# Staging rows of a decayed-attention layer: interleaved rows with flat stores, maxima in two transfers, and a layer norm one step earlier

## Reference

```
x = x + 0.5 * moe(layernorm(x))      # 8 experts, the best 2
x = x + attention(layernorm(x))      # 16 heads of 8 features
x = x + 0.5 * moe(layernorm(x))

# attention, per head: q, k, v = x@Wq, x@Wk, x@Wv
c      = cumsum(log_sigmoid(x @ Wf))          # one number per head and token
scores = q k^T * 8**-0.5 + c[i] - c[j], causal
out    = softmax(scores) @ v, heads joined, @ Wo
```

## Time and profile before

| | us |
|---|---|
| median of 3 runs | 488.97 |
| lowest, highest | 486.0, 489.73 |
| the profiled execution, its own time | 487.24 |
| its span, first to last instruction | 485.5 |
| PE busy in the span | 416.7 |
| DVE busy | 372.5 |
| ACT busy | 278.3 |
| POOL busy | 239.7 |

### The profile page before, as it was taken

The page is one execution under the profiler, slowest core; times in us unless marked ns, Lnnn a source line. Parts: engine busy times, 40 slices in busy tenths (PEclk is TensorE's granted clock), DMA queues, the critical chain, the costliest instruction groups (busy, mean ns, idle before and its releaser), DMA issues.

```text
span 485.5 us, 12085 instructions
## 1 busy us (share of the span) xinstructions
PE 416.7 (86%) x3472; PEld 303.6 (63%) x3488; DVE 372.5 (77%) x1316; ACT 278.3 (57%) x758; POOL 239.7 (49%) x397
## 2 busy tenths in 40 slices
PE   1888887847799999999999999999989999888884
PEld 0656566526556766676676676676667666566662
DVE  4999999874856865876785686676576658999995
ACT  5676766440354555565556466455555685666753
POOL 8955566351425534533543543553442543566554
PEclk9999999895989999999999999999999999999999
DMA  3311000033333333234233233323322000001101
GB/s 108 92 52 20 1 0 1 8 99 109 101 98 101 94 100 115 73 96 114 69 104 102 85 96 100 100 84 98 111 77 80 4 3 0 24 24 32 33 22 43
DMA packets 29402, 32.47 MB, mean 67 GB/s; under 512 B 2312, under 2 KB 26140, under 8 KB 29370
## 3 DMA queue, kind: packets, MB, share of 16 engines
q1 hardware_dynamic: 28282, 31.57, 22.1%
q10 hardware_dynamic: 1088, 0.52, 0.4%
HBM read 16.05 MB, written 15.20 MB: 64 GB/s over the span
## 4 chain that ended last, share of the span: by engine, by line
PE 40%; DVE 22%; DMA 19%; issue 10%; ACT 3%; POOL 3%; DVEq 1%; SPq 1%; ACTq 0%; POOLq 0%; another core or an unknown queue 0%
DMA a_q_rows<-a_max_t 16%; PE bank L847 10%; PE bank L862 7%; DVE m_lower L288 7%; PE bank L877 6%; PE bank L850 3%; PE bank L968 2%; PE bank L960 2%; PE bank L963 2%; DVE m_stats L335 2%; DMA q_stage<-a_q_parts 2%; POOL m_pair L216 2%; DVE x_all L297 2%; DVE m_best_no L376 2%; PE bank L886 1%
## 5 line engine op out<-in xcount | busy, mean ns | idle before, releaser
L773 DVE TENSOR_REDUCE a_neg_max<-bank 128x2 f32<-128x512 f32 (+1 forms) x192 | 124.3, 687 | 76.2 <-PE bank L850 70.2
L712 ACT ACTIVATE a_weights<-bank 128x512 f32<-128x512 f32 x192 | 108.4, 592 | 60.5 <-PE bank L862 55.6
L658 POOL TENSOR_SCALAR_AFFINE_SELECT a_weights<-a_weights 128x512 f32<-128x512 f32 (+1 forms) x96 | 75.7, 790 | 127.9 <-ACT a_weights L712 127.7
L847 PE MATMUL bank<-a_k_rows,a_q_rows 104*128 104x256 f32 (+1 forms) x512 | 100.9, 321 | 7.7 <-DMA a_k_rows<-k_stage 6.5
L847 PEld LDWEIGHTS bank<-a_k_rows,a_q_rows 104*128 104x128 f32 x512 | 78.9, 199 | 26.9 <-issue 18.5
L246 ACT ACTIVATE m_scaled<-bank,m_gates 128x128 f32<-128x128 f32 x256 | 72.6, 367 | 25.0 <-PE bank L417 25.0
L862 PE MATMUL bank<-a_q_rows,a_k_rows 106*128 106x512 f32 (+1 forms) x192 | 69.8, 442 | 11.1 <-DMA a_q_rows<-a_max_t 10.5
L216 POOL TENSOR_TENSOR m_pair<-m_scaled 128x256 f32<-128x256 f32 x64 | 48.3, 755 | 60.4 <-ACT m_scaled L246 60.1
L288 DVE SCALAR_TENSOR_TENSOR m_lower<-bank,m_gates,m_lower 128x128 f32<-128x128 f32 x192 | 66.1, 344 | 1.2
L877 PE MATMUL bank<-a_weights,a_v 128*32 128x128 f32 x1536 | 61.6, 279 | 0.0
L850 PE MATMUL bank<-a_mask,a_ident 128*128 128x256 bf16 (+1 forms) x176 | 56.4, 321 | 0.0
(11 more groups left out here) (126 smaller groups left out, 784.0 us busy)
## 6 DMA issues: line engine op xcount, KB each, us to landing
a_k_rows<-k_stage SPq DMA_DIRECT2D x16, 416.0 KB
k_stage<-a_k_parts SPq DMA_DIRECT2D x48, 128.0 KB
q_stage<-a_q_parts SPq DMA_DIRECT2D x48, 128.0 KB
a_q_rows<-q_stage SPq DMA_DIRECT2D x64, 96.0 KB
x_all<-in_L_attn_x SPq DMA_DIRECT2D x8, 256.0 KB, 2.8
out_x<-x_all SPq DMA_DIRECT2D x8, 256.0 KB, 2.3
we<-in_L_ffn_We SPq DMA_DIRECT2D x1, 512.0 KB, 4.0
k_stage<-a_c_parts SPq DMA_DIRECT2D x32, 16.0 KB
```

What stands on the lines that cost most here:

```text
L658: nc.gpsimd.affine_select(out=diagonal, in_=diagonal, compare_op=ALU.is_ge, fill=0.0, base=0, pattern=[[0, heads.stop - heads.start], [1, P]],
L712: nc.scalar.activation(weights[n // 2 % 3][:, half:half + 4, :].rearrange("p h n -> p (h n)"), wt_bank[n % 2][:, :], ACT.Exp).then_inc(wt_ ...
L773: nc.vector.tensor_reduce(neg_max[:, t, first:first + heads], score_bank[p % 2][:, :].rearrange("p (h n) -> p h n", h=heads), AX.X, ALU.ma ...
L847: nc.tensor.matmul(bank[:, n * keys:(n + 1) * keys], q_rows[b][0:KR, h, t * P:(t + 1) * P], k_rows[b][0:KR, h % NU, 0:keys], start=n == 0, ...
```

## The change

1. **Layout.** The staging tensors have the row outermost and the group second, and rows of the groups are interleaved in `q_rows` and `k_rows` (row r of group g is partition 4r + g). The weights Wq and Wk are reordered to match (d, g, u instead of g, d, u). A store is then 128 partitions to one flat piece of DRAM, a c store 16 partitions to one flat piece. The loads of `q_rows` write every fourth partition. Sizes and numbers of stores and loads stay.
2. **Maxima.** `send_max` issues two DMAs, one for each of the two rows, each from 16 partitions (16 heads). The waits count 32 in place of 16.
3. **Layer norm.** Statistics and power of a sequence move from part 0 of step s to part 3 of step s-1, `xn` from part 1 to part 4 of step s-1. Sequence 0 stays where it was. In part 3 of DVE's list the statistics stand behind the two row maxima and ahead of L813 and `normalise`; in part 4 `xn` stands behind the two row maxima, ahead of L819 and L821. POOL's power stands behind `causal` of part 3.
4. **xT.** In part 2 ACT's copy to `xt` stands ahead of exp number 4.
5. **Loop.** For all engines but SP the loop is three rounds (steps 2 to 10); steps 11 to 13 are written out.

```diff
-    run_steps(..., 0, seqs - 1, (2, 2 + (seqs - 4) // 3 * 3), 3)
+    run_steps(..., 0, seqs - 1, (2, 2 + (seqs - 5) // 3 * 3), 3)
...
-    q_dram = nc.dram_tensor("q_stage", (3, NG, 3 * HD, NU, N), FP32, kind="Internal").ap()
-    k_dram = nc.dram_tensor("k_stage", (3, NG, ROWS, NU, N), FP32, kind="Internal").ap()
+    q_dram = nc.dram_tensor("q_stage", (3, 3 * HD, NG, NU, N), FP32, kind="Internal").ap()
+    k_dram = nc.dram_tensor("k_stage", (3, ROWS, NG, NU, N), FP32, kind="Internal").ap()
...
-                    sp.dma_start(raw(q_rows[b])[ROWS * g:ROWS * g + 3 * HD, NU * g:NU * (g + 1), :],
-                                 q_dram[b, g]).then_inc(rows_in, 16)
+                    sp.dma_start(raw(q_rows[b])[g:NG * 3 * HD:NG, NU * g:NU * (g + 1), :],
+                                 q_dram[b, :, g]).then_inc(rows_in, 16)
...
-                    sp.dma_start(k_dram[b, :, r * HD:(r + 1) * HD].rearrange("g d u n -> g (d u) n"),
+                    sp.dma_start(k_dram[b, r * HD:(r + 1) * HD].rearrange("d g u n -> (d g u) n"),
                                  raw(k_parts)[:, part, :]).then_inc(k_stored, 16)
...
-                    sp.dma_start(k_dram[b, :, 3 * HD + part], raw(c_parts)[:, part, :]).then_inc(c_stored, 16)
+                    sp.dma_start(k_dram[b, 3 * HD + part].rearrange("g u n -> (g u) n"), raw(c_parts)[:, part, :]).then_inc(c_stored, 16)
...
-            if j == 0 and 0 <= s + 2 < NSEQ:
-                n = i + 3
-                pool.wait_ge(eps_done, n)
-                nc.gpsimd.tensor_tensor(rstd[:, :], var_eps[:, :], c["minus_half"][:, 0:2], ALU.pow).then_inc(rstd_done, 1)
+            if s == -2 and j == 0:
+                rstd_of(i + 3)
+            if j == 3 and 0 <= s + 3 < NSEQ:
+                rstd_of(i + 4)
...
-            act.dma_start(raw(q_rows[s % 3])[KR:KM, :, t * P:(t + 1) * P], raw(max_t[t])).then_inc(max_in[t], 16)
+            for k in range(2):
+                act.dma_start(raw(q_rows[s % 3])[KR + k:KR + k + 1, :, t * P:(t + 1) * P],
+                              raw(max_t[t])[k * H:(k + 1) * H, :]).then_inc(max_in[t], 16)
...
-            if X:
-                exp(i - 1, s - 1, 2 * j)
             if j == 2 and F:
                 act.wait_ge(xt_ready, n)
                 nc.scalar.activation(xt[:, :], proj_bank[:, 0:N], ACT.Copy).then_inc(xt_copied, 1)
+            if X:
+                exp(i - 1, s - 1, 2 * j)
...
+            if s == -2 and j == 0:
+                dve.wait_ge(before["tiles_done"], 2)
+                statistics(i + 2, n)
+            if s == -2 and j == 1:
+                normalised(i + 2, n)
+            if j == 3 and 0 <= s + 3 < NSEQ:
+                if s <= 0:
+                    dve.wait_ge(before["tiles_done"], 2 * (s + 4) if s < 0 else 2 * NSEQ)
+                statistics(i + 3, n + 1)
+            if j == 4 and 0 <= s + 3 < NSEQ:
+                wait_apart(dve, xt_ready, n, dve_waited)
+                normalised(i + 3, n + 1)
...
-                pe.wait_ge(max_in[0], (i + 1) * 16)
+                pe.wait_ge(max_in[0], (i + 1) * 16 * 2)
```

More of the change, by code:

```diff
@@ L64, in run_layers @@
     beside("amamammaaa", -1, moe1, groups - 1)
-    run_steps(eng, lambda i, s: [attention(i, s, k) for k in range(6)], 0, seqs - 1, (2, 2 + (seqs - 4) // 3 * 3), 3)
+    run_steps(eng, lambda i, s: [attention(i, s, k) for k in range(6)], 0, seqs - 1, (2, 2 + (seqs - 5) // 3 * 3), 3)
     beside("amaamamaam", seqs - 1, moe2, -2)
@@ L505, in attention_layer @@
     c_parts = sb("c_parts", [H, 2, N], FP32R)
-    wq_gdu = sb("wq_gdu", [P, D], FP32)
-    wk_gdu = sb("wk_gdu", [P, D], FP32)
+    wq_dgu = sb("wq_dgu", [P, D], FP32)
+    wk_dgu = sb("wk_dgu", [P, D], FP32)
     ones_row = sb("ones_row", [H, N], FP32)
@@ L571, in constant_rows @@
             for g in range(NG):
-                sp.dma_start(raw(q_rows[b])[ROWS * g + 3 * HD:ROWS * (g + 1), NU * g:NU * (g + 1), :], ones).then_inc(ones_in, 16)
+                sp.dma_start(raw(q_rows[b])[NG * 3 * HD + g:KR:NG, NU * g:NU * (g + 1), :], ones).then_inc(ones_in, 16)
             sp.dma_start(raw(k_rows[b])[KR:KM, :, :], ones).then_inc(ones_in, 16)
@@ L598, in step @@
                 for r, part in enumerate((0, 1, 0)):
-                    sp.dma_start(k_dram[b, :, r * HD:(r + 1) * HD].rearrange("g d u n -> g (d u) n"),
+                    sp.dma_start(k_dram[b, r * HD:(r + 1) * HD].rearrange("d g u n -> (d g u) n"),
                                  raw(k_parts)[:, part, :]).then_inc(k_stored, 16)
                 for r, part in enumerate((0, 0, 1)):
-                    sp.dma_start(q_dram[b, :, r * HD:(r + 1) * HD].rearrange("g d u n -> g (d u) n"),
+                    sp.dma_start(q_dram[b, r * HD:(r + 1) * HD].rearrange("d g u n -> (d g u) n"),
                                  raw(q_parts)[:, part, :]).then_inc(q_stored, 16)
@@ L660, in causal, with rstd_of @@
                                     channel_multiplier=-1).then_inc(wt_causal, 1)
+        def rstd_of(n):
+            pool.wait_ge(eps_done, n)
+            nc.gpsimd.tensor_tensor(rstd[:, :], var_eps[:, :], c["minus_half"][:, 0:2], ALU.pow).then_inc(rstd_done, 1)
         def split_max(i, s, t):
@@ L691, in order_columns @@
         act.wait_ge(made["small_in"], 16 * 6)
-        for ordered, name in ((wq_gdu, "Wq"), (wk_gdu, "Wk")):
-            nc.scalar.activation(ordered[:, :].rearrange("p (g d u) -> p g d u", g=NG, u=NU),
-                                 c[name][:, :].rearrange("p (g u d) -> p g d u", g=NG, u=NU), ACT.Copy).then_inc(w_ordered, 1)
+        for ordered, name in ((wq_dgu, "Wq"), (wk_dgu, "Wk")):
+            nc.scalar.activation(ordered[:, :].rearrange("p (d g u) -> p d g u", g=NG, u=NU),
+                                 c[name][:, :].rearrange("p (g u d) -> p d g u", g=NG, u=NU), ACT.Copy).then_inc(w_ordered, 1)
     def scalar(act):
@@ L699, in copy_max @@
             act.wait_ge(max_t_ready, i * 2 + t + 1)
-            at_least(act, max_in[t], i * 16)
+            at_least(act, max_in[t], i * 16 * 2)
             nc.scalar.activation(max_t[t][:, :], side_bank[0:2 * H, 0:P], ACT.Copy).then_inc(max_copied, 1)
@@ L775, in row_max, with statistics, normalised @@
                                     AX.X, ALU.max, negate=True).then_inc(max_done, 1)
+        def statistics(q, n):
+            for t in range(2):
+                last = nc.vector.bn_stats(stats[:, t], tile(q * 2 + t))
+            last.then_inc(stat_done, 1)
+            wait_apart(dve, stat_done, n, dve_waited)
+            for t in range(2):
+                last = nc.vector.bn_aggr(moments[:, t], stats[:, t])
+            last.then_inc(mom_done, 1)
+            dve.wait_ge(mom_done, n)
+            nc.vector.tensor_scalar(var_eps[:, :], moments[:, :, 1], EPS, None, ALU.add).then_inc(eps_done, 1)
+        def normalised(q, n):
+            dve.wait_ge(rstd_done, n)
+            for t in range(2):
+                last = nc.vector.tensor_scalar(xn[:, t], tile(q * 2 + t), moments[:, t, 0:1], rstd[:, t:t + 1],
+                                               ALU.subtract, ALU.mult)
+            last.then_inc(xn_done, 1)
         def normalise(i, s, t):
@@ L792, in part @@
                 row_max(i, s, 2 * j + 1)
-            if j == 0 and F:
-                if s <= 0:
[L795 to L810, removed]
+            if s == -2 and j == 0:
[4 more added lines that the diff above has]
+            if j == 3 and 0 <= s + 3 < NSEQ:
+                if s <= 0:
+                    dve.wait_ge(before["tiles_done"], 2 * (s + 4) if s < 0 else 2 * NSEQ)
[3 more added lines that the diff above has]
+                normalised(i + 3, n + 1)
             if j == f_part(s) + 1 and F:
@@ L854, in turned_scores @@
             if n == 0:
-                pe.wait_ge(max_in[0], (i + 1) * 16)
+                pe.wait_ge(max_in[0], (i + 1) * 16 * 2)
             if n == 4:
-                pe.wait_ge(max_in[1], (i + 1) * 16)
+                pe.wait_ge(max_in[1], (i + 1) * 16 * 2)
             at_least(pe, wt_exp, i * 12 + n - 1)
@@ L962, in part @@
                 pe.wait_ge(f_copied, n)
-                nc.tensor.matmul(q_ps, wq_gdu[:, :], xt[:, :], start=True, stop=True)
-                nc.tensor.matmul(k_ps, wk_gdu[:, :], xt[:, :], start=True, stop=True).then_inc(qk_ready, 1)
+                nc.tensor.matmul(q_ps, wq_dgu[:, :], xt[:, :], start=True, stop=True)
+                nc.tensor.matmul(k_ps, wk_dgu[:, :], xt[:, :], start=True, stop=True).then_inc(qk_ready, 1)
             if j == 5 and T:
```

2 lines of the change are left out of this document (1 added, 1 removed).

## The result

| | before | after |
|---|---|---|
| median, us | 487.49 (4 runs, 483.54 to 489.73) | 472.21 (4 runs, 470.08 to 474.8) |
| ratio, 95% interval | 1 | 0.9698 [0.9644, 0.9752] |
| the profiled execution, its own time | 487.24 | 470.08 |
| its span | 485.5 | 468.3 |

The changed kernel is 3.0% faster, and the forecast was 472. Total and range held. The experiments give a different account of what each part contributed.

The account below looks back on a forecast made before the run. The prediction took PE to set the step, busy 16.79 of 17.50 us. Its terms summed to -16.2, from 487.24 to 471.0, moved to 472 for the spread of the runs; range 465 to 481.

Parts of the forecast that it names:

- -10.5: Steady steps: PE's 0.75 us wait for the maxima goes in each of 14 steps, saving 10.5 us.
- Rival B: Flat stores stay on four engines, or the one-partition write holds up the maxima: 478 to 479 us, chance 0.08.
- rival E: Loads that begin earlier collide with the second maxima: 510 us, chance 0.05 together with rival D.
- xT, -2.0: Part 2: with the copy ahead of exp 4, `xt` is there before PE asks, saving 2.0 us.
- First rows, -2.6: Start: first stores land sooner, so first row loads come earlier despite the norm ahead; 2.6 us saved, bounds 0 and 3.7.
- -1.5: PE's one wait for `xn` goes, as `xn` is written a step ahead: 1.5 us saved.
- +0.7: Step 0: `xn` in part 4 lies on the path, since there is little PE work: 0.7 us lost.
- Two transfers, costed at nothing: ACT, parts 0 and 3: the second maxima DMA adds 0.62 us of issue between exps, priced at 0.
- rival D: Slower: `xn` waits for POOL's power, behind `causal` of part 3 and the second issue; 498 us, chance 0.05 together with rival E.
- +1.4: Steady steps: residual waits from the moved norm, 0.1 us in each of 14 steps, 1.4 us lost.
- rival C: The wait moves: PE stands for DVE in parts 3 to 5, 0.5 us a step; 477 us, chance 0.12.
- Clock, -1.7: Stretch behind the `xn` wait, PE's clock at 0.51 of full: without the gaps, 1.7 us saved.

Follow-up runs that it names:

- e8: The kernel before with only the new layout and its flat stores: 470.10 us, ratio 0.9634 to the kernel before.
- e1: The changed kernel with q and k stores written with outermost DRAM dimension 4, an edit that changed nothing in effect: 470.73 us, ratio 0.9690 to the kernel before.
- e4: The changed kernel with ACT's `xt` copy behind exp 4 again: 474.07 us, ratio 0.9750 to the kernel before, step 16.85.
- e6: The changed kernel with the norm back in parts 0 and 1 and the maxima in one transfer: 464.94 us, ratio 0.9555 to the kernel before.
- e9: The kernel before with only the maxima sent in two transfers: 487.87 us, ratio 1.0017 to the kernel before.
- e3: The changed kernel with the norm back in parts 0 and 1: 480.85 us, ratio 0.9872 to the kernel before, step 17.38.
- e2: The changed kernel with the maxima sent in one transfer again: 469.16 us, ratio 0.9644 to the kernel before.
- e5: The changed kernel with the old layout, group outermost, all else kept: 489.56 us, ratio 1.0058 to the kernel before.
- e12: e6 with the loop of the kernel before, four rounds (twelve steps): 464.79 us, ratio 0.9526 to the kernel before.

## Why the prediction was right, and where it wasn't

**The stores' traffic was the cause of the late maxima: right, and the size too small.** e8 changes the layout alone, and the time goes. The term was -10.5, 0.75 a step. From the first to the last second maxima the kernel before takes 388.97 - 128.86 = 260.11, e8 372.42 - 126.57 = 245.85: 14.3 less, 0.95 in each of 15 steps. The prediction priced the wait by PE's row; the weight load's row has the same wait longer (6.4 in seven waits, 0.91 each), and the step goes by the longer one here. Rival B is out: landing 1.8, share 0.58. So is rival E: the loads go out at 243.48, 1.7 after the maxima's issue, and these still land in 1.9. The rule of the Trainium skill (DMA: Bandwidth & Descriptors, "Why a DMA increments its semaphore by 16 and not by 1") agrees with the shares, though no run here varied the number of engines by itself, as e1 missed.

**xT, -2.0: right in kind, too small** for the same reason. 0.30 a step (e4) to 0.37 (e8 to e6), some 4 to 5 us in all; PE's row had 0.18, the weight load's 0.42.

**First rows, -2.6: right in kind.** The prediction let the first stores land in 2.3 in place of the chain's 8.40, charged 2.4 for the norm of sequence 1 ahead of them, and so had the first scores at most 3.7 earlier. They came 6.1 earlier, and 5.5 earlier in e8, which leaves the norm where it was: the stores land in 1.8, and in the changed kernel the first of them goes out only 0.7 later (94.98 for 94.27), not 2.4. How much of this the norm takes back stays open, since the starts of like programs differ by 1.9 (e1) to 3.2 us (e9). At the first second maxima 3.8 are left, near the sum of the terms for the start (-2.6, -1.5 and +0.7).

**Two transfers, costed at nothing: wrong.** The prediction looked for cover in part 3 and found it. It named the issue in part 0 and priced nothing there, where the second issue delays exp 1, then `causal`, the power and `xn`, which PE wants in part 2. This is rival D's mechanism in another part, with a price of about 1.1 a step (e3 to e6). The norm's move hides it: with it, one transfer or two differ by 0.08 a step (e2). The gain they were to bring is the stores' alone.

**Norm, -1.5 and "leaving gains nothing in a steady step":** the 1.5 for `xn` went. The rest holds with one transfer alone, where the move costs 0.21; e3 shows 0.83 gained with two. The **+1.4** for residual waits (rival C, in small) was right in kind and half the size, 13 x 0.21 = 2.7, and it shows at `turn_max` and not at L951.

**Clock, -1.7: wrong.** The half-clock stretch moved and stayed, and another came near the end. The table of stretches of the changed kernel:

```profile
373.02:380.02 7.00, 6.84 (x71) 4.55 (x72) 2.70 (x20) 5.80 (x14) 4.16 (x7) 0.80 0.01 4
124.00:128.00 4.00, 3.84 (x17) 3.15 (x16) 2.23 (x5) 1.46 (x3) 2.68 (x4) 0.59 0.42 139
128.00:132.00 4.00, 4.00 (x20) 3.21 (x23) 1.98 (x3) 1.97 (x5) 1.63 (x4) 0.56 0.50 149
```

In e1, in effect the same program, the clock was 1.00 in all three stretches, and instead 0.50 from 112 to 116; of the 1.8 us by which its span is shorter 1.3 lie behind the last maxima. So most of what the changed kernel lost between its last maxima and the end isn't the change's. Over the whole span the granted clock is 0.981 before and 0.983 after, and 0.969 to 0.984 in the four runs of the changed kernel: no gain is shown. Which gap draws the clock down isn't settled.

So the total is right in good part by luck: two terms that were too small (the maxima by 3.8, xT by 2 to 3) met others that weren't there or were left out (the clock's 1.7, the norm's steady cost, a little for the second transfer, and the 1.8 lost at the end).

## What to carry to other kernels

A wait of a matmul can stand in two rows, its own and that of its weight load. They are one wait, so don't add them: the cost here lay between the two, or near the longer one (0.30 to 0.37 for `xt`, with 0.18 and 0.42; 0.95 for the maxima, with 0.75 and 0.91). Best compare the length of a step. When a small transfer comes late, look at the DMA share while the large ones beside it run before splitting the small one: its second issue is time on the issuing engine, and all that hangs on that engine's next instruction moves with it. And when several edits come together, run the ones without which it might do as well: here one of the four parts hid the damage of another, and the kernel without both is faster. Before a difference at the start of a kernel is put down to an edit, look at two profiles of one program.

## What the runs showed of the hardware

- **Issue time depends on the transfer's shape.** The timeline of SP in the changed kernel:

```profile
239.02 1.44 SPq L602 DMA_DIRECT2D q_stage<-a_q_parts  x3
242.00 0.78 SPq L606 DMA_DIRECT2D k_stage<-a_c_parts  x2
243.48 2.97 SPq L590 DMA_DIRECT2D a_q_rows<-q_stage  x4
```

  A store takes 0.48 to issue where it took 0.76, a c store 0.39 for 0.80, but a load of `q_rows`, now from rows apart in DRAM to every fourth partition, 0.74 for 0.38. SP has room for it here.
- **Two small transfers beside slow stores** landed in 3.8 (e9) and 4.1 us (e5), medians, against 1.9 in the changed kernel. Each is quicker than the single one's 5.50, but the second is issued some 0.6 later, and from the first issue to the last landing e5 takes 5.27.
- **The clock at the start differs between like kernels**: e12 has 1.00 in all stretches from 104 to 136 us, e6, which differs in the loop alone, 0.50 from 112 to 124. It differs between executions of one kernel too: the six of e6 have 0.975 to 0.991 over the whole span.
